# A decoder layer on one core: the projection stage written out in a planned order, and the x2 store of cross attention two turns later

## The reference, cut to what matters

```
q = silu(dwconv(hs @ Wq, conv_q))            # dwconv: causal, 4 taps, per feature
k = silu(dwconv(hs @ Wk, conv_k))
v = silu(dwconv(hs @ Wv, conv_v))
beta = sigmoid(hs @ Wb)
q, k = l2norm(q), l2norm(k)                  # per head of 64 features
attn = -(k * beta) @ k.T ...                 # Gram matrices of k, scaled by beta
...
x = layernorm(x + cross_attention(ctx, x))   # its result x2 goes to the experts
```

## Time and profile before

| | us |
|---|---|
| median of 3 runs | 1736.34 (1734.69 to 1737.81) |
| the profiled execution | 1727.94 |
| span in its profile | 1726.1 |
| projection stage, first DMA to the next stage's first | 13.7 to 310.3 |
| cross attention, first DMA to the next stage's first | 800.2 to 1212.1 |
| busy in the span: PE / DVE / ACT / POOL | 1460.0 / 911.7 / 680.1 / 592.5 |

### The profile page before, as it was taken

One profiled execution on the slowest core, in us unless ns is written; L12 is line 12 of the kernel. 1 busy time (PEld: TensorE's weight loads), 2 busy tenths in 40 slices (PEclk: granted clock), 3 DMA queues, 4 the chain that ended last, 5 costly groups with the idle time before them and its releaser, 6 DMA issues. The chain is left out here.

```text
span 1726.1 us, 26013 instructions
## 1 busy us (share of the span) xinstructions
PE 1460.0 (85%) x8444; PEld 1142.4 (66%) x8445; DVE 911.7 (53%) x1708; ACT 680.1 (39%) x1293; POOL 592.5 (34%) x476
## 2 busy tenths in 40 slices
PE   4876775599599999984999898998897999999995
PEld 1554454599588888863878787887475666666643
DVE  3665664795289999982543433444651122212277
ACT  3322230399577767761233323334102222222214
POOL 3665456100144555552222212112123444444310
PEclk9776775555699999996999989999898999999998
DMA  5255332544433333312211221111402111111154
GB/s 135 68 152 141 97 97 85 166 137 130 140 107 101 88 90 86 107 34 85 80 45 52 82 74 61 55 56 50 136 1 71 56 56 55 58 55 58 49 191 132
DMA packets 148713, 151.86 MB, mean 88 GB/s; under 512 B 63936, under 2 KB 115744, under 8 KB 147744
## 3 DMA queue, kind: packets, MB, share of 16 engines
q1 hardware_dynamic: 111648, 108.95, 21.6%
q10 hardware_dynamic: 30080, 23.07, 4.2%
q0 software_dynamic: 6912, 18.88, 3.3%
HBM read 98.43 MB, written 42.99 MB: 82 GB/s over the span
## 5 line engine op out<-in xcount | busy, mean ns | idle before, releaser
L2346 DVE TENSOR_TENSOR hidden<-unit_psum,gate 128x352 f32<-128x352 f32 x72 | 37.8, 525 | 210.3 <-ACT gate L2309 210.3
L1759 POOL TENSOR_TENSOR scores<-scores,score_max 128x1024 f32<-128x1024 f32 x32 | 60.7, 1897 | 256.7 <-DVE score_max L1687 256.7
L642 PE MATMUL fir_psum<-window,toep 96*96 96x128 f32 x512 | 116.6, 401 | 23.6 <-DMA toep<-in_fir 21.8
L655 ACT ACTIVATE filtered<-fir_psum 32x512 f32 (+1 forms) x192 | 112.7, 587 | 47.3 <-PE fir_psum L642 42.7
L642 PEld LDWEIGHTS fir_psum<-window,toep 96*96 96x96 f32 x512 | 111.7, 257 | 28.5 <-DMA window<-value 20.3
L2277 PE MATMUL unit_psum<-wd,hiddenT 128*128 (+1 forms) x432 | 112.0, 395 | 13.9 <-issue 12.6
L334 PE MATMUL proj_psum<-xT_block,wqkv 128*128 128x512 f32 x192 | 97.9, 664 | 25.6 <-DMA xT_block<-in_xT 22.2
L467 DVE SCALAR_TENSOR_TENSOR conv_acc<-proj_psum,conv_taps,conv_acc 128x508 f32<-128x508 f32 (+1 forms) x144 | 96.2, 736 | 38.4 <-ACT conv_acc L389 38.4
L2208 POOL DMA_INDIRECT unit_rows<-x_rows,token_of_slot x72 | 69.9, 971 | 127.0 <-PE unit_psum L2251 104.5
L2215 POOL DMA_INDIRECT outs<-unit_out,choice_of_slot x72 | 71.1, 987 | 99.5 <-DVE unit_out L2351 96.8
L2277 PEld LDWEIGHTS unit_psum<-wd,hiddenT 128*128 128x128 f32 (+1 forms) x432 | 76.4, 190 | 36.5 <-issue 28.7
(11 more groups left out here) (283 smaller groups left out, 3428.7 us busy)
## 6 DMA issues: line engine op xcount, KB each, us to landing
gate_part<-in_gw1s SPq DMA_DIRECT2D x8, 1280.0 KB, 10.7
ndg<-decay_gram ACTq DMA_DIRECT2D x8, 1024.0 KB, 8.1
neg_decay_gram<-ndg SPq DMA_DIRECT2D x16, 512.0 KB, 3.6
ctxT_tiles<-in_ctxT SPq DMA_DIRECT2D x16, 512.0 KB, 4.4
gathered<-outs SPq DMA_DIRECT2D x32, 256.0 KB, 2.8
window<-value SPq DMA_DIRECT2D x32, 192.0 KB, 2.9
toep<-in_fir SPq DMA_DIRECT2D x64, 96.0 KB, 2.1
xT_block<-in_xT SPq DMA_DIRECT2D x8, 512.0 KB, 5.7
```

The source lines that it names most:

```text
L642: mm = pe.matmul(psum[0:NFIR * QUART, u, TC * w + c, :], toep[:, w, :, :, c].rearrange("p f t -> p (f t)"), window[:, u, :, :, TC * w + c] ...
L655: act.activation(M.filtered[q * QUART:(q + 1) * QUART, f, bass.ds(n, 1), :, :].rearrange("p k b c -> p (k b) c"), psum[f * QUART:(f + 1) * ...
L1759: pool.tensor_tensor(sc[:, i % 2, t, :, :], sc[:, i % 2, t, :, :], wide(mx[:, t, :], [128, XH, L], 2), ALU.subtract).then_inc(shifted[t], 1)
```

## The change

The hardware loop of the projection stage goes; `unrolled` writes out all turns on every engine, each with its own list. Tiles are handled in pairs p = 0, 1, 2 (q, k, v) with one semaphore each, ACT's Silu and POOL's square take a pair in one instruction, each pair uses two PSUM banks in turn, and a block's work is spread over turns n to n+2. POOL keeps `gate_rows`, between the squares and `inverse_norms`. The stores move from ACT's queue to SP's. In cross attention `store` is called for unit n-6 in place of n-4.

```diff
-            staged_pair_loop(act, NBLK, (convolved, 0), (store_qk, 0), (small, 1), (store_decays, 2))
-            skewed_pair_loop(pe, NBLK, projections, derived)      # and dve, pool alike
+        def pair_bank(n, p, m):
+            return 2 * ((PAIRS * n + p) % 2) + m
 @block.sync
+            def load_x(n):
+                if n >= 2:
+                    sp.wait_ge(small_mm, n - 1)
+                    sp.wait_ge(proj_mm[2], n - 1)
...
+            def load_gate(n):
+                sp.wait_ge(gate_step, n)
...
+            unrolled(NBLK, (load_gate, 1), (store_qk, 3), (load_x, 0), (store_decays, 3))
 @block.tensor
+            def projections(p):
...
+                    before = PAIRS * n + p - 2
+                    if before >= 0:
+                        pe.wait_ge(conv_done[before % PAIRS], before // PAIRS + 1)
...
+            def grams(g):
+                def step(n):
+                    pe.wait_ge(silu_done[1], n + 1)
+                    pe.wait_ge(gram_scaled[1 - g], n + g)
...
+            unrolled(NBLK, (projections(0), 0), (grams(0), 2), (small, 1), (projections(1), 0), (grams(1), 2),
+                     (turn_values(0), 1), (projections(2), 0), (turn_values(1), 1))
 @block.scalar
+                    act.activation(qkv[:, u, 2 * p:2 * p + 2, :], conv[:, 2 * p:2 * p + 2, :], ACT.Silu)...
...
+            unrolled(NBLK, (scaled_taps(0), 0), (silus(2), 1), (tanhs, 1), (keep_values(1), 2), (scaled_taps(1), 0),
+                     (keep_values(0), 1), (silus(0), 0), (silus(1), 0), (scaled_taps(2), 0))
 @block.vector
+            def decays(n):
+                u, here = n % 2, slice(BB * n, BB * n + BB)
+                dve.wait_ge(tanh_done, n + 1)
+                dve.wait_ge(norms_done, n + 1)
...
                 dve.tensor_scalar(tanh_b[:, u, :, :], tanh_b[:, u, :, :], 0.5, 0.5, ALU.mult,
                                   ALU.add).then_inc(decay_step, 1)
-                dve.wait_ge(norm_done, n + 1)
                 dve.tensor_copy(M.rq[:, here, :], ssq[:, u, :, 0:H])
                 dve.wait_ge(decay_step, 3 * n + 1)
...
+            unrolled(NBLK, (convolutions(0), 0), (keep_squares, 1), (convolutions(1), 0), (scale_grams(1), 2), (decays, 1),
+                     (convolutions(2), 0), (scale_grams(0), 1))
 @block.gpsimd
+                    pool.tensor_tensor(squares[:, u, 2 * p:2 * p + 2, :], qkv[:, u, 2 * p:2 * p + 2, :],
+                                       qkv[:, u, 2 * p:2 * p + 2, :], ALU.mult).then_inc(squared[p], 1)
...
+            unrolled(NBLK, (square(0), 0), (square(1), 0), (gate_rows, 0), (inverse_norms, 0))
 # cross attention, SP
-            for n in range(2, UNITS + 4):
+            for n in range(2, UNITS + 6):
                 if n < UNITS:
                     load(n)
-                if n >= 4:
-                    store(n - 4)
+                if n >= 6:
+                    store(n - 6)
                 load_expert(n - 2)
```

More of the change, by code:

```diff
@@ new lines, in project @@
+        small_mm = sem("small_mm")
+        tanh_step = sem("tanh_step")
+        tanh_done = sem("tanh_done")
+        ssq_kept = sem("ssq_kept")
+        norms_done = sem("norms_done")
+        decay_step = sem("decay_step")
+        decay_done = sem("decay_done")
+        vT_mm = [sem(f"vT_mm{g}") for g in range(2)]
+        v_kept = [sem(f"v_kept{g}") for g in range(2)]
+        gram_mm = [sem(f"gram_mm{g}") for g in range(2)]
+        gram_scaled = [sem(f"gram_scaled{g}") for g in range(2)]
@@ L323, in _ @@
-            pair_loop(sp, NBLK, load_x)
+            unrolled(NBLK, (load_gate, 1), (store_qk, 3), (load_x, 0), (store_decays, 3))
+            for u in range(2):
+                sp.wait_ge(qk_stored[u], 32 * (NBLK // 2))
+                sp.wait_ge(nd_stored[u], 16 * (NC + 1) * (NBLK // 2))
         @block.tensor
         def _(pe):
[L327 to L336, removed]
@@ L440, in _, with scaled_taps, step @@
-            staged_pair_loop(act, NBLK, (convolved, 0), (store_qk, 0), (small, 1), (store_decays, 2))
-            for u in range(2):
-                act.wait_ge(qk_stored[u], 32 * (NBLK // 2))
-                act.wait_ge(nd_stored[u], 16 * (NC + 1) * (NBLK // 2))
+            def scaled_taps(p):
+                def step(n):
+                    act.wait_ge(proj_mm[p], n + 1)
+                    act.wait_ge(silu_done[p], n)
+                    for m in (2 * p, 2 * p + 1):
+                        act.activation(conv[:, m, :], psum[:, pair_bank(n, p, m % 2), :], ACT.Copy,
+                                       scale=taps[:, m // KD, m % KD, TAPS - 1:TAPS]).then_inc(taps_scaled[p], 1)
+                return step
@@ new lines, in silus, with step @@
+            def silus(p):
+                def step(n):
+                    u = n % 2
+                    act.wait_ge(conv_done[p], n + 1)
+                    if n >= 2:
+                        if p < 2:
+                            act.wait_ge(qk_stored[u], 32 * (n // 2))
+                            act.wait_ge(squared[p], n - 1)
+                            act.wait_ge(gram_mm[0], n - 1)
+                            act.wait_ge(gram_mm[1], n - 1)
+                        else:
+                            act.wait_ge(vT_mm[0], n - 1)
+                            act.wait_ge(vT_mm[1], n - 1)
+                    act.activation(qkv[:, u, 2 * p:2 * p + 2, :], conv[:, 2 * p:2 * p + 2, :], ACT.Silu).then_inc(silu_done[p], 1)
+                return step
```

254 lines of the change are left out of this document (117 added, 137 removed).

## The result

The changed kernel takes 1651.4 us (median of 4 runs, 1649.46 to 1653.98); the kernel before took 1735.5 beside it (4 runs, 1734.66 to 1737.81). The ratio is 0.9514, with a 95% interval of 0.9498 to 0.9531. Forecast were 1653 us, within 1616 to 1680. The profiled execution took 1649.46 us, its span 1647.8.

A forecast was written before the change was run, and what follows sets the result against it. A chain of waits, not an engine, bounds the projection stage; in cross attention, a store delays context loads. 1736.3 less 45 (projection) and 38 (cross attention) gives 1653 us, own range 1640 to 1668, wider range 1616 to 1680.

The forecast's parts named there:

- the fourth is caught by gate rows: Projection block: DVE's fourth of five chained decay operations stands still until POOL's gate rows end, at p+17.5 us.
- rival A: Projection stage: decay operations are not caught, two or three slip through each gap; PE sets 24 us, 1628 us; chance 0.24.
- The block, 28.5 forecast: Projection block: loop closed through gate rows, from last decays to gate rows, sums to 28.5 us, where 34.2 were.
- PE's own path fits inside: Projection block: k products start at half clock (5.5 us); k's taps end at 15, its square due at 17.5.
- The start and the drain: Projection stage: block 2's square ends at 81.8, five blocks of 28.5 follow, stage ends at 264.6 us, not 310.3.
- Stores on SP: Projection stage: moving stores to SP's queue costs 0, or up to 8.1 us a block if the cover is gone.
- written-out code: Projection stage: unrolling the loop costs nothing as counted; -2 to +5 us allowed for fetching the code.
- Cross attention, -38 forecast: Store of unit n-6 ends the idle before keys: 223.5 us for ten turns, -38 us, between -28 and -45.
- the first hold: Cross attention: the first delay of keys behind a store, 898.3 to 901.3 us; removing it adds 3 us of gain.
- B: Projection stage: PE stays at half clock and becomes the bound, 37 us a block, 1695 us; chance 0.07.
- C: Cross attention gains nothing because another wait takes the store's place, 1691 us; chance 0.08, with halves of it.
- D: Projection stage: SP's one queue serves transfers strictly one after another, `load_x` waits behind stores, 1810 us; chance 0.03.

The follow-up runs named there:

- the quarters: Changed kernel with each gate rows addition on POOL cut into four instructions of 2 rows: 1628.1 us, ratio 0.940.
- e9: Changed kernel with the stores of q, k and the scaled Grams back on ACT's queue, loads alone on SP's: 1649.0 us, ratio 0.952.
- e2: Kernel before the change with only the cross attention store moved to unit n-6: 1700.9 us, ratio 0.980.
- halves: Changed kernel with each gate rows addition on POOL cut into two instructions of 4 rows: 1646.5 us, ratio 0.949.

## Why the prediction was right

**The hold.** The step "the fourth is caught by gate rows" was right in place and kind: in 6 of the stage's blocks `decay` is the one held, to the end of gate rows. What no row had shown before, a square holding a decay operation, is there too (1.82 us up to the end of k's square), so rival A's way out by that door was closed. Cutting the instruction opened it, and the block then fell to the 24.0 us that rival A had for PE, with 1628 us, the time that it gave. One reading of the forecast was too generous: in the block of the earlier trace rows three of the 18 taps run beside gate rows, not "many"; that taps are not held is shown better by the quarters, where v's six (137.66 to 141.64) run wholly beside the adds (133.04 to 142.35) in 3.98 us.

**The block, 28.5 forecast, 27.36 measured.** The loop from gate rows' start, term by term from the timelines above, with the forecast in brackets: gate rows 8.82 (8.85), last decay 0.16 (0.4), v's taps 3.90 (4.0), scaling 1.19 (1.3), q's taps 3.90 (4.0), copy 0.26 (0.2), norms 5.40 (5.5), two squares 3.73 (4.2). Every member is there. The mis-sized terms are the merged square, 1.88 for 2.1 us, and the last decay, one operation where two were counted; the rest is a tenth here and there, since an instruction in a chain starts about 0.1 before the record of the one ahead ends.

"PE's own path fits inside" held narrowly: the forecast left 1.4 us between k's Silu and its square (15 + 1.1 against 17.5 us after gate rows), and 0.1 was left (16.5 against 16.6), because the products of k ran at half clock, 6.4 us for 5.5. PE's total came out (24.3 for 22.9, or about 24 with part at half clock), but partly by luck in its terms: the two Grams take 2.3 us for 4.2 and v 1.3 for 2, the head sums 7.9 for 6.2 and the products 13.6 for 10.5, as more of both ran at half clock.

**The start and the drain.** Squares of k end at 38.5, 60.8 and 84.4 us (39.6, 59.3, 81.8 forecast). The blocks of the start were longer than forecast because head sums take 7.7 to 7.9 us, not 6.2: half of them run at half clock. From there: 84.4 + 5 x 27.36 = 221.2, gate rows to 230.0, last norms to 241.0, stage end 260.64 (264.6 forecast). Against 264.6 that is 4.0 us less: the squares and the small overlaps make 5.7 (5 x 1.14), the late start takes back 2.6, and the drain gives the rest. The stage gained 49.6 us for 45.

**Stores on SP, written-out code.** The first cost nothing, as taken, by `e9`. The second was not tested by itself: a stage whose loop can be summed to 27.36 of 27.36 us from its members leaves little room for it in the steady blocks.

**Cross attention, -38 forecast, -32.1 measured.** The mechanism was right: the ten turns behind the first hold take 225.6 us (223.5 forecast), 6 of them with a fall of the clock (4 of 10 taken) but 21.55 long without (21.65 taken), and the first hold gave its 3.0. Over the eleven turns that is -36.2. The step that failed is one that I didn't make: I took the drain behind the last keys as unmoved, and it took 4.5 us more, at a grant of 0.86 for 0.94. The two errors, 4.6 too little and 5.9 too much, nearly cancelled: -81.7 for -83. The untouched stages added 3.5 to the profiled execution (1649.5), and the median lies 1.9 above that, not the 8.4 carried over from before; so 1651.4 for 1653 is closer than the sum was.

**The rivals.** B (PE at half clock all through): the grant is 0.75 and PE idles. C (no gain in attention): refuted by `e2`, 34 us. D (SP's queue): PE waits for no `xT_block` after the first, and `e9` gains nothing. A needed an edit of its own.

## What to carry to other kernels

When small operations of one engine stand still beside another's instructions, look at what each stands beside, not only at its length: an operation of 0.2 us cost 8.75 here, and cutting the long instruction on the other engine (or moving the small ones behind what others wait for) was worth 20 us with the arithmetic unchanged. Of a chain of small operations that wait for one another, one passed at each boundary between the adds, so halves gave nothing and quarters everything that PE left to gain.

An edit that fills an engine's idle time or mends its clock is safe only if it leaves the order along the loop of waits alone; four kernels with a better-looking order on PE lost 19 to 24 us in the stage, because an instruction in the loop (the second head sums, the Grams) now stood behind others on PE that had been outside it.

## What the runs showed of the hardware that was not expected

- TensorE's grant fell from 1.00 to 0.51 in the midst of a block's 48 narrow products (2 and 4 columns), which follow one another and the Grams without a gap: 26 instructions in 2.70 us, the next 26 in 5.19. In cross attention it fell in 6 of 11 otherwise equal turns, in the queries behind 32 products of 33 columns.
- Sixteen Gram products of 64 rows take 1.16 us at full clock; the 2.08 of the earlier trace rows, which the forecast used for all, were at half clock (grant 0.50 from 238.9 to 240.9 us).
- POOL's memset of 8.09 us holds a DVE multiply by a constant to its end (7.79 us) and lets a multiply of two SBUF tiles through in 0.17, in five blocks. Two taps behind the held multiply start before it ends (136.61 against 144.3) and are done by 144.4.
- The same drain of 316 to 318 PE instructions took 52.1 to 61.6 us in four kernels, at grants of 0.94 to 0.77.
